# High and low parts of rotated queries, keys and values made where they are produced, and loaded as parts in attention

## The reference

```
q = (query @ wq).reshape(bs, sq, HQ, DK).transpose(0, 2, 1, 3)
k = (key @ wk).reshape(bs, sk, HKV, DK)
v = (value @ wv).reshape(bs, sk, HKV, DV)
...
q = apply_rope(q, pos)
k = apply_rope(k, curr_seq_pos + jnp.arange(sk))
scores = jnp.einsum('bhqd,bhkd->bhqk', q, k) / scale
attn = jax.nn.softmax(scores + m[:, None, :, :], axis=-1)
out = jnp.einsum('bhqk,bhkd->bhqd', attn, v)
out = out.transpose(0, 2, 1, 3).reshape(bs, sq, HQ * DV)
return out @ wo
```

## Time and profile before

| | before |
|---|---|
| median of 3 runs | 1972.09 us |
| the profiled execution: its span, taken as its own time | 1970.4 us |
| PE busy | 1869.6 us (95%) |
| DVE, ACT, POOL busy | 57%, 32%, 32% |
| DMA | 188.70 MB, mean 96 GB/s |
| query phase, PE busy | 191.0 us, 169.2 |
| key phase | 270.6 us, 265.4 |
| layer-0 phase | 416.4 us, 401.0 |
| second query phase | 322.9 us, 316.7 |
| attention | 685.1 us, 648.7 |
| final phase | 84.4 us, 68.6 |

### The profile page before, as it was taken

One profiled execution on the slowest core, in us unless ns is written; L12 is line 12 of the kernel. 1 busy time (PEld: TensorE's weight loads), 2 busy tenths in 40 slices (PEclk: granted clock), 3 DMA queues, 4 the chain that ended last, 5 costly groups with the idle time before them and its releaser, 6 DMA issues. The chain is left out here.

```text
span 1970.4 us, 30192 instructions
## 1 busy us (share of the span) xinstructions
PE 1869.6 (95%) x9628; PEld 1676.1 (85%) x9628; DVE 1116.1 (57%) x2473; ACT 630.0 (32%) x1337; POOL 623.7 (32%) x427
## 2 busy tenths in 40 slices
PE   5999999998999999979999997899999999999997
PEld 5998999996777777769999987898898989889985
DVE  6631556563222222246666657877777777777766
ACT  2212211022222222221111114565555656565612
POOL 2324522144222222022222233442534434343413
PEclk9999999998999999989999998999999999999998
DMA  3112433245333333222333243232222323232403
GB/s 119 57 61 80 142 99 110 78 135 171 112 113 114 112 113 114 80 76 80 101 104 102 102 140 108 72 100 70 86 72 80 94 65 105 61 91 75 133 3 101
DMA packets 137953, 188.70 MB, mean 96 GB/s; under 512 B 41320, under 2 KB 107432, under 8 KB 137872
## 3 DMA queue, kind: packets, MB, share of 16 engines
q1 hardware_dynamic: 137872, 187.80, 31.1%
HBM read 141.14 MB, written 46.63 MB: 95 GB/s over the span
## 5 line engine op out<-in xcount | busy, mean ns | idle before, releaser
L202 PE MATMUL bank<-shared_operand_high,w_first_high 128*128 128x448 f32 (+1 forms) x768 | 279.4, 364 | 14.7 <-issue 4.9
L202 PE MATMUL bank<-shared_operand_low,w_first_high 128*128 128x448 f32 (+1 forms) x768 | 278.7, 363 | 0.0
L202 PE MATMUL bank<-shared_operand_high,w_first_low 128*128 128x448 f32 (+1 forms) x768 | 278.6, 363 | 0.0
L1354 ACT ACTIVATE e_scores<-e_scores,e_nmax 112x375 f32<-112x375 f32 x256 | 155.1, 610 | 154.9 <-DVE e_nmax L1347 154.3
L202 PE MATMUL bank<-e_o_t_high,e_wo_high 128*128 128x448 f32 x512 | 195.4, 382 | 1.3 <-DVE e_o_t_low L1532 1.3
L202 PE MATMUL bank<-e_o_t_high,e_wo_low 128*128 128x448 f32 x512 | 189.2, 369 | 0.0
L202 PE MATMUL bank<-e_o_t_low,e_wo_high 128*128 128x448 f32 x512 | 188.9, 369 | 0.0
L279 POOL TENSOR_TENSOR shared_operand_low<-ctx_raw,shared_operand_high 128x752 fp32r<-128x752 f32 x64 | 116.3, 1830 | 207.0 <-ACT shared_operand_high L275 207.0
L202 PEld LDWEIGHTS bank<-shared_operand_high,w_first_high 128*128 128x128 f32 x768 | 145.8, 190 | 26.8 <-issue 5.4
L1343 DVE CUSTOM_DVE_ANT_0 e_scores<-bank,e_mask 112x375 f32<-112x375 f32 x256 | 139.8, 546 | 40.8 <-issue 23.0
L1324 POOL TENSOR_TENSOR e_v_low<-e_raw_v,e_v_high 125x384 fp32r<-125x384 f32 x64 | 65.5, 1023 | 287.7 <-ACT e_v_high L1313 287.7
(11 more groups left out here) (173 smaller groups left out, 4185.5 us busy)
## 6 DMA issues: line engine op xcount, KB each, us to landing
ctx_raw<-in_ctx_t SPq DMA_DIRECT2D x64, 376.0 KB, 3.6
e_raw_wo<-in_wo SPq DMA_DIRECT2D x32, 512.0 KB, 5.2
aw_weights_then_ctx_rows<-in_wq SPq DMA_DIRECT2D x30, 512.0 KB, 3.5
q_rotated<-q_rotated_then_x_rows SPq DMA_DIRECT2D x64, 224.0 KB, 1.9
e_raw_q<-q_rotated SPq DMA_DIRECT2D x64, 224.0 KB, 2.8
k_rotated<-k_rotated_sb SPq DMA_DIRECT2D x64, 188.0 KB, 1.9
e_raw_k<-k_rotated SPq DMA_DIRECT2D x64, 188.0 KB, 2.7
aw_weights_then_ctx_rows<-in_ctx_nat SPq DMA_DIRECT2D x8, 1500.0 KB
```

The source lines that it names most:

```text
L202: mm = pe.matmul(out, stationary[a], moving[b], start=(first and i == 0), stop=(last and i == 2))
L1354: act.activation(self.s_buf[:, t, h, :], self.s_buf[:, t, h, :], ACT.Exp, bias=self.nm[:, t, h:h + 1], accum_out=self.total[:, t, h:h + 1] ...
```

## The change

The stores of k, v and q in DRAM now hold both parts of each number, high and low. They are made where the tensors are produced: in the key phase by ACT (`head_high`) and POOL (`head_low`) for each head, in the layer-0 phase by ACT and DVE for each piece of v, in the second query phase by ACT and POOL for each unit. The buffers of rotated heads shrink from four to two, and two or four buffers of parts are new. The attention steps load q, k and v as parts, straight into the operands of PE (448, 376 and 375 KB a step instead of 224, 188 and 187.5), and the three copies on ACT and three subtractions on POOL of a step are gone. The value weights' low parts move from POOL to DVE, between its heads. The loads' conditions change: q and k of step s+2 wait for the scores of step s, v of step s+2 for `o_acc` of step s.

```
 key phase, SP
-            load_ctx(BATCH - 1, BATCH - 1)
+            batch(LAST - 1, LAST)
             load_ctx(BATCH, 0, (0, 1))
             for c in range(3):
                 load_wv(c)
-            store(BATCH - 2)
+            store(LAST, (0,))
             load_ctx(BATCH, 0, (2, 3))
-            for g in range(GROUPS):
-                store_head(BATCH - 1, g)
-                if g + 3 < CH:
-                    load_wv(g + 3)
+            for g in range(1, GROUPS):
+                store_head(LAST, g)
+                if 3 <= g + 2 < CH:
+                    load_wv(g + 2)
...
 key phase, ACT, POOL and DVE
+            def head_high(b, g):
+                act.wait_ge(ready, GROUPS * b + g + 3)
+                act.wait_ge(stored[g % 2], 16 * (GROUPS // 2 * b + g // 2) + 16)
+                act.activation(parts[:, g % 2, 0, :], rotated[:, g % 2], ACT.Copy).then_inc(key_high, 1)
+            def head_low(b, g):
+                pool.wait_ge(key_high, GROUPS * b + g + 1)
+                pool.tensor_tensor(parts[:, g % 2, 1, :], rotated[:, g % 2], f32(parts[:, g % 2, 0, :]),
+                                   ALU.subtract).then_inc(key_low, 1)
...
+                    dve.wait_ge(key_low, n + 1)
+                    dve.tensor_tensor(rotated[:, g % 2], straight[:, g % 2], crossed[:, g % 2],
+                                      ALU.add).then_inc(ready, 1)
+                    if known(b) and b == LAST and g >= 1:
+                        value_weight_low(g - 1)
...
 second query phase, SP, ACT, POOL
-                sp.wait_ge(ready, unit + 3)
+                sp.wait_ge(head_low, unit + 3)
...
             first.load(sp)
             head_pair(LAST - 1, True)
-            first.load_next(sp)
             head_pair(LAST, False)
...
+            def high(unit, i, t, h):
+                act.wait_ge(ready, unit + 3)
...
+            def low(unit, t, h):
+                pool.wait_ge(head_high, unit + 1)
...
 attention
     def load_qk(self, sp, s, b, g):
         if not (known(s) and s < 2):
-            sp.wait_ge(self.qk_low, 2 * s - 2)
+            sp.wait_ge(self.scored, 4 * s - 4)
...
     def load_v(self, sp, s, b, g):
         if not (known(s) and s < 2):
-            sp.wait_ge(self.v_low, s - 1)
-        sp.dma_start(self.raw_v[:, b % 2], self.k.v_dram[b, :, :, bass.ds(P * g, P)].rearrange(
-            "c p d -> p c d")).then_inc(self.v_in[b % 2], 16)
+            sp.wait_ge(self.o_acc, s - 1)
+        sp.dma_start(f32(self.v_both[:, b % 2]), self.k.v_dram[b, g]).then_inc(self.v_in[b % 2], 16)
...
     def load(self, sp):
         sp.dma_start(self.mask[:, :, :], self.k.mask.rearrange("b q s -> q b s")).then_inc(self.mask_in, 16)
-        self.load_qk(sp, 0, 0, 0)
-        self.load_qk(sp, 1, 1, 0)
-        self.load_v(sp, 0, 0, 0)
+        for b in range(2):
+            self.load_qk(sp, b, b, 0)
+            self.load_v(sp, b, b, 0)
...
 attention, SP's step
-                if not (last and s + 3 >= STEPS):
-                    first.load_qk(sp, s + 3, (u + 3) % 8, g + (u + 3) // 8)
                 if not (last and s + 2 >= STEPS):
+                    first.load_qk(sp, s + 2, (u + 2) % 8, g + (u + 2) // 8)
                     first.load_v(sp, s + 2, (u + 2) % 8, g + (u + 2) // 8)
                 if u < 4:
                     load_wo(u, g, known(s))
```

More of the change, by code:

```diff
@@ L602, in store_head, with store @@
             def store_head(b, g):
-                sp.wait_ge(ready, GROUPS * b + g + 3)
-                sp.dma_start(k.kt_dram[b, g], rotated[:, g % 4]).then_inc(stored[g % 4], 16)
-            def store(b):
-                for g in range(GROUPS):
+                sp.wait_ge(key_low, GROUPS * b + g + 3)
+                sp.dma_start(k.kt_dram[b, g], f32(parts[:, g % 2])).then_inc(stored[g % 2], 16)
+            def store(b, gs=range(GROUPS)):
+                for g in gs:
                     store_head(b, g)
@@ L1405, in attention_phase @@
         s_buf, v = first.s_buf, first.v
-        turned, normed, o_acc, v_low = first.turned, first.normed, first.o_acc, first.v_low
+        turned, normed, o_acc, v_in = first.turned, first.normed, first.o_acc, first.v_in
         wo_in = [sem(f"e_wo_in{i}") for i in range(2)]
@@ L1452, in step @@
                 more = not (last and s + 1 >= STEPS)
-                if not (last and s + 2 >= STEPS):
-                    first.qk_high_part(act, s + 2, (u + 2) % 8)
                 for c in range(KEY_TILES):
@@ L1478, in step @@
             def step(s, u, g):
-                last = known(s) and s >= STEPS - 4
-                if not (last and s + 2 >= STEPS):
-                    first.qk_low_part(pool, s + 2, (u + 2) % 8)
-                if not (last and s + 1 >= STEPS):
-                    first.v_low_part(pool, s + 1, (u + 1) % 8)
                 if u < 4:
```

283 lines of the change are left out of this document (157 added, 126 removed).

## The result

| | before | after |
|---|---|---|
| median of 4 runs each, on one chip | 1971.71 us | 2123.88 us |
| the profiled execution's span | 1970.4 us | 2123.9 us |
| DMA read, written | 141.1, 46.6 MB | 180.4, 85.9 MB |
| query phase | 191.0 | 191.9 |
| key phase | 270.9 | 299.1 (+28.2) |

The change makes the kernel slower: ratio 1.0765 [1.073, 1.08], +152 us where +43 was forecast, and outside the range. The phases are cut at PE's first instruction of each. Attention was to bring +24 and brought 91; each of the other three gave several times its term or nearly twice it.

What follows compares the result with a forecast made beforehand. PE, busy 95% of the span, was taken as the bound. Attention +24, key phase +10, layer 0 +2 and second queries +7 gave +43 on 1970.4; with 1.7 for the median 2015, rounded to 2016; own range 1996 to 2055, 8-in-10 1983 to 2056.

Steps and rivals of the forecast that it cites:

- Attention: Attention phase: normalising gain -25, wo stalls +35, first group +8 and slower PE clock +6, in all +24 us.
- The wo wait: Attention: ACT open for wo's landing, 2.5 us stalls in seven groups +35, first group +8, lower PE clock +6.
- The bound of 6.8: Attention: upper bound of wo's landing in us, making a stall of 4.1, +45 at the worst.
- The normalising: Attention: normalising at its own speed without POOL's subtractions, 13.7 us at six loop starts, 11.2 in first four steps: -25.
- The wider loads: Attention: q, k and v of 1199 KB a step instead of 600 cost nothing unless they slow wo: 0.
- Key phase: End of key phase: last batch's context tiles issued about 439.5, so PE starts the next phase at 472, not 462.02: +10.
- Layer 0: Layer-0 phase: ACT, POOL and DVE have slack; first tiles and weights come a little late: +2 (0 to 5).
- Second query phase: Its end: 1.42 MB more ahead of a weight load, 5.1 us, and 1.7 before the barrier: +7 (2 to 12).
- (a): Attention: wo wait mostly absorbed, landing at 4.4 or less, stall 1 us: +10 in total, 1982; chance 0.15.
- (b): Attention: wo as cheap as q and k, landing below 3, nothing lost, -25 stays: near 1956; chance 0.08.
- (c): Key and second query phases: POOL's new subtractions meet DVE's sums; +25 on top in the query loop, 2041; chance 0.17.

Runs made afterwards that it cites:

- wo ahead: Changed kernel with the wo part issued ahead of the step's loads of q, k and v in attention: 2036.07 us, ratio 1.0293.
- Both mends of it: Changed kernel, key phase: next batch's first context tiles loaded after the fourth key store (2112.38 us, 1.0692); separately, four buffers of key parts (2118.23 us, 1.0736).
- the three mends: Changed kernel with wo issued ahead, key-phase context tiles loaded earlier, and a late second-query weight load put ahead of attention's loads: 2006.46 us, 1.0179.
- the late weight's mend: Second last weight load of the second query phase issued ahead of attention's loads, run only together with two other edits to the changed kernel: 2006.46 us, 1.0179.
- its repeat: Same kernel as the three mends, since a further edit's condition was never true: 2005.24 us, 1.0169.
- the kernel with the quiet POOL: Kernel before, with ACT making v's high part ahead of the last two exponentials and POOL waiting for the normalising after v's low part: 1932.48 us, 0.9812.

## Why the prediction was wrong, point by point

**The wo wait (+35, +8, +6): mechanism right, the landing and the clock mis-sized.** The failing sentence is "I take the median, since only v runs beside it as before". v does not run beside wo but ahead of it, and was doubled: 6.8, not 5.2, and 7.3 with q and k behind. The bound of 6.8 stood in the working, with +45 at the worst. By the chain counted there a landing of 7.3 makes the first stall 2.5 + 2.1 = 4.6; measured are 5.1. The steps that were to absorb the next wait do not: the second, third and fourth lose 2.8, 2.7 and 5.2 too, the last with a turn in it. Counted 49, measured 88. The clock was mis-sized too: 0.7 us a stall, +6, where PE's busy time grew by 38 us. An estimate from the granted clock, 0.07 of 776 us less 0.03 of 685, is 34 us of clock withheld more than before. With wo ahead of v, landing at 3.8, the same chain gives 2.5 - 1.4 = 1.1, measured are 1.4, and the second step of a group loses nothing, as counted.

**The normalising (-25): the row is right, the gain is not there.** All of them are at 1.39. In the first four steps most of the 11.2 us went to the wider q and k, which land late: steps 1 to 5 take 54.2 us with wo ahead and 58.5 before, so 4.3 came. At the turns nothing came: the extra there was 6.1 us before, of which the normalising's step is 2.2; the rest, 3.9, comes in the next step, behind DVE's gap, in which the instructions' own transfer waits for the one of v. With a v twice as large the gap grew from some 4.0 to 6.0 to 6.5, and the turn costs 5.7 without any lock; 1.6 a group more are waits for q and k. The prediction read the earlier trace rows and stopped at the first of two stalls. The step periods would have shown both.

**The wider loads (0): wrong.** A mean of 125 GB/s is no limit, but each load has a place in a line of transfers, and it was read as if only bandwidth counted. This step of the prediction is behind the errors in all phases.

**Key phase (+10): place right, size 28.** The period of a head in the last batch was 3.3 us (3.7 counted). What failed is "now it is about 439.5": the last batch's tiles are issued at 449.0, since every batch already ends late: two buffers, a store of twice the size behind loads, and tiles behind the store. Both mends of it help (16 and 11 us).

**Layer 0 (+2): 20.5.** "ACT, POOL and DVE have slack" is true and beside the point: it put the transfers at nothing. ACT waits for the value stores, 500 KB each in two buffers (119.3 us, before 0), and longer for tiles (71.0 us, before 24.3), both beside 1500 KB of rows a batch. With a third of these rows the loss is gone, and both waits with it; which of the two costs PE the time stays open.

**Second query phase (+7): 12.5.** 1.42 MB were to cost 5.1 us; PE's wait grew from 2.55 to 12.30, that is by 9.8. The barrier behind the last store grew by 1.9, as counted (1.7).

**The rivals.** (a) and (b), a short landing, fell with 7.3 us; with wo ahead of v it lands at 3.8, and the wait then costs 10 us, where (a) had counted 18, so the rival was about right on what a short landing is worth. The sum of (a) is wrong by 2: 14 + 4 - 25 + 19 is +12, not +10. (c) did not decide: the query sum has a mean of 742 ns, less than the 1246 of the earlier trace rows, and in the whole second query phase PE waits only for the late weight (12.3 us) and at the barrier (7.4).

```profile
L1314 DVE TENSOR_TENSOR q_rotated_then_x_rows<-q_straight,q_crossed 128x448 f32<-128x448 f32 x64 | 47.5, 742 | 18.9 <-POOL q_rotated_then_x_rows L1271 16.8
```

**Open.** The wait for a wo that lands at 3.8 costs 34 us in one profile of the kernel before (27 by the ratio) and 10 in the changed one (8 by the ratios). The first stall of a group is 2.3 us there and 1.4 here. That the copies of q and k, which stand on ACT between wo's copy and those of p_t in the kernel before (0.57 and 0.50 us), make the difference is argued, not shown. Of the three mends' 36 us over before, the key phase and layer 0 hold most, and no kernel with stored parts was found that is faster than before. Of the second query phase's 12.5 us, 6.5 came back with the late weight's mend in one run and 1.9 in its repeat.

## What to carry to other kernels

Work moved from an engine with idle time into transfers is paid where a transfer's landing is waited for: before such a change, list for each load what is issued ahead of it and who stands open on it. In a loop of like steps take the differences of one instruction's starts over all steps first; whatever is over the regular period is the whole account, and each excess wants its own cause. And when an engine that is not the bottleneck costs time by holding another, move its work, and the loads that wait for it, by a few us before removing it: that gave -37 us here (26 of them by an order on ACT that lets v's load leave sooner), and removing it +152.

## What the runs showed of the hardware

- A transfer's landing goes by what is ahead of it on its issuing engine: 512 KB of wo take 3.8 us alone, 5.2 behind 187 KB, 6.8 behind 375 KB; 824 KB behind it add only 0.5 (7.3). The Trainium skill ("DMA: Bandwidth & Descriptors", section "Queues, rings and completion order") says that on each DMA engine descriptors are consumed in ring order. The runs agree.
- At each turn of the attention loop DVE stands with nothing to wait for: 2.6 to 2.9 us with no transfer in flight, 3.6 to 4.3 behind a v of 187 KB, 5.7 to 6.5 behind one of 375 KB, 2.6 to 2.7 again when this v is held back. In each gap one packet of 8192 bytes runs on the instruction queue; it starts 0.5 to 0.8, 1.2 to 1.9, 3.5 to 4.0 and 0.5 us into these gaps, and they end 2.1 to 2.6 us behind its start. The Trainium skill ("Runtime: NRT & Kernel Launch", section "Instruction fetch mechanics") says that a taken branch whose target is out of the window forces a fetch by DMA before execution goes on. The gaps and the packets agree with that, and these runs add that the fetch starts the later, the more data is under way.
- PE takes longer for the same matmuls where it stalls more often: 687.0 us busy at a granted clock of 0.93 in the changed attention phase, 649.1 at 0.97 with wo ahead, 637.0 at 0.99 in the kernel with the quiet POOL.
- Pieces of 4096 or of 1024 bytes in a store of 500 KB made no difference (ACT waits 117.8 and 119.3 us for these stores, and the whole time is the same within the interval).
